# A graph layer and sparse experts kernel: tile 0 selected ahead of the tables, the third tile's W1 loaded early, the first layer in halves of W1

## The chip, the cores and the metric

One core of a Trainium2 chip. The metric is device time in microseconds (us) of one execution, the median of three runs. "The trace" is that of one profiled execution of the kernel before.

## The reference, cut

625 rows of 512 features go through four steps, each on a layer norm of the sum so far and added to it: a graph convolution over 20,000 edges with a linear layer, a small fixed network on a few columns, three graph layers of 512 x 512, and last the part that matters here, a routed network of 16 experts:

```python
for d in range(4):                       # a tree of depth 4 gives each row one of 16 experts
    sel = take_along_axis(xf @ Wr[off:off + cnt].T + br[off:off + cnt], leaf[:, None], 1)[:, 0]
    leaf = leaf * 2 + (sel > 0)
...
h = gelu(xf @ w1 + bb1)                  # W1: 16 x 512 x 2048
y = h @ w2 + bb2                         # W2: 16 x 2048 x 512
acc = acc + m[:, None] * y               # m: the rows of this expert
```

## The kernel before

Five engines run their own instruction lists and wait on semaphores; nothing is planned at run time but what follows. One expert's W1 and W2 are 4 MB each, float32. The kernel computes each expert for its own rows only. A **tile** is one expert with up to 64 rows, and one expert of the 16, the one with the most rows, may have 96 (`more`, tile 14, with matmuls of its own, `first_b` and `second_b`). With these inputs there are 16 tiles, in pairs `p`, `b`; the last pair stands behind the loop. Tiles 0 and 1 are always experts 0 and 1 (`FIXED`), so their weights are loaded at the start of the program; which expert the later tiles are stands in a table (`tab`, `s_table`) that VectorE works out from the routing.

Ahead of tile 0 VectorE ranks the rows by expert, works out the table, and from each row's rank the place of each row, from which `sel` (L1259, semaphore `s_sel`) selects tile 0's 64 rows: TensorE multiplies it with the normed rows (L885), VectorE copies them (L1306), TensorE transposes them (L878, `turn_rows`), VectorE copies the result (L1301, `copy_inputs`). The rows of the later tiles are fetched by GpSimd with a gather from a copy in DRAM (L426). It needs row numbers, `rows_i` (`s_idx`), which come from maps of slots on VectorE (L1308 to L1319), 40 small matmuls on TensorE (L894) and nine steps on VectorE (to L1328).

A tile on TensorE: first layer (L913), 16 matmuls into two PSUM banks, `h` 0 and 1, two for each bank and each of the four row blocks `k` of W1 (the trace counts a float32 matmul as two); transposes of the hidden values (L930) after VectorE's copy (L1338); bias (L947); transposes of the next tile's rows (L878); second layer (L961) in quarters `q`, each behind GELUs on ScalarE (L599). ScalarE copies the result (L611) and GpSimd adds it to the output with a scatter (L433), for which it first picks the row numbers (L420).

There are two buffers for W1 and W2 (`w1_sb`, `w2_sb`). SyncE issues four loads of 2 MB a tile, in order: the two halves `j` of W1, the two halves of W2, each as soon as the tile that used this buffer, two tiles earlier, has read that half (`s_w1u`, `s_h`, `s_l2`). All go through one queue.

The functions that the diff touches, as they stood:

Of the kernel before, what the change touches and what calls it, by code (L numbers as in the profile page):

```python
# [62 lines left out]
FIXED = 2  # L63
# [7 lines left out]
def build(nc, x, src, dst, Wconv, bconv, Wlin, blin, Wa, ba, Ws, bs, Wg, bg, Wr, br, W1, b1, W2, b2, out):  # L71
    ctx = ExitStack()
    with ctx:
# [110 lines left out]
        in_tile = C[:, :, :].rearrange("p c n -> p (c n)")[:, 0:(TAB + 2) * NCH].rearrange("p (t c) -> p t c", c=NCH)  # L184
        tok_tile = C[:, :, :].rearrange("p c n -> p (c n)")[:, 160:160 + (TAB + 2) * NCH].rearrange("p (t c) -> p t c", c=NCH)
        slots = C[:, :, :].rearrange("p c n -> p (c n)")[:, 320:320 + NCH * SA].rearrange("p (c s) -> p c s", c=NCH)
        slotsB = C[:, :, :].rearrange("p c n -> p (c n)")[:, 640:640 + NCH * SB_].rearrange("p (c s) -> p c s", c=NCH)
        rows_f = C[:, :, :].rearrange("p c n -> p (c n)")[:, 960:960 + 3 * (TAB + 2)].rearrange("p (a t) -> p a t", a=3)
        rows_i = C[:, :, :].rearrange("p c n -> p (c n)")[:, 1060:1060 + 3 * (TAB + 2)].bitcast(I32).rearrange("p (a t) -> p a t", a=3)
        row_in, row_inB, row_outB, *row_out = (C[:, :, :].rearrange("p c n -> p (c n)")[:, 920 + i:921 + i].bitcast(I32) for i in range(5))  # L190
        row_inB = row_inB[0:2 * SB_, :]
        half_ofB = C[:, :, :].rearrange("p c n -> p (c n)")[:, 940:941]
        spos = C[:, :, :].rearrange("p c n -> p (c n)")[:, 930:930 + NCH]
# [3 lines left out]
        b1_nat = G[0:2 * NE, 0:HID // 2]  # L197

        b1T = G[:, 1536:1536 + NE * (MH + 1)].rearrange("p (e m) -> p e m", e=NE)
        b1T_flat = G[:, 1536:1536 + NE * (MH + 1)]  # L200
        bT = [G[:, 1824 + b * (MH + 1):1824 + (b + 1) * (MH + 1)] for b in range(2)]
        b2_rows = G[:, 1024:1024 + DIM]
# [19 lines left out]
        s_w1 = [sem(f"w1_in{b}") for b in range(2)]  # L222
# [53 lines left out]
        def _(sp):  # L276
# [41 lines left out]
            for b in range(2):  # L318
                for j in range(2):
                    sp.dma_start(w1_sb[b][:, 2 * j:2 * j + 2, :],  # L320
                                 W1[b, j * 256:(j + 1) * 256, :].rearrange("(p r) n -> p r n", r=2)).then_inc(s_w1[b], 16)
# [18 lines left out]
            sp.dma_start(b1_nat, b1.rearrange("e (h n) -> (e h) n", h=2)).then_inc(s_b1, 16)  # L340
# [12 lines left out]
            with sp.Fori(0, last) as p:  # L353
                for b in range(2):
                    done = 2 * p + b + 1
                    e = sp.value_load(tab[0:1, bass.ds(done + 1, 1)], min_val=0, max_val=NE - 1)
                    for j in range(2):
                        if j == 0:
                            sp.wait_ge(s_w1u, (done - 1) * (KD - 1) + 2)
                        else:  # L360
                            sp.wait_ge(s_h, done * 2)
                        sp.dma_start(w1_sb[b][:, 2 * j:2 * j + 2, :],
                                     W1[bass.ds(e, 1), j * 256:(j + 1) * 256, :].rearrange("a (p r) n -> p (a r) n", r=2)).then_inc(s_w1[b], 16)
                    for h in range(2):
                        sp.wait_ge(s_l2, 4 * (done - 1) + 2 * h + 2)
                        sp.dma_start(w2_sb[b][:, 8 * h:8 * h + 8, :],
                                     W2[bass.ds(e, 1), h * HID // 2:(h + 1) * HID // 2, :].rearrange("a (p m) n -> p (a m) n", p=128)).then_inc(s_w2[b][h], 16)
# [256 lines left out]
        def _(pe):  # L624
# [277 lines left out]
            def tile(p, b, end=False):  # L902
# [476 lines left out]
```

## Time and profile before

| | |
|---|---|
| three runs, us | 628.8, 629.48, 632.06; median 629.48 |
| profiled execution, us | 632.86 |
| its span, first to last instruction, us | 630.9 |
| TensorE matmuls busy | 549.9 us, 87% of the span |
| VectorE, ScalarE, GpSimd busy | 191.2, 162.4, 62.1 us |
| mean granted TensorE clock | 0.96 |
| read from HBM | 142.38 MB |

The span is the program's own time, and the time of an execution is measured around it. Busy shares are averages over stages of very different kinds: the graph steps up to about 285 us, the routing up to 312 us, and the tiles.

### The profile page before, as it was taken

What the parts mean: (1) busy time and instruction counts of PE and PEld (TensorE: products, weight loads), DVE (VectorE), ACT (ScalarE), POOL (GpSimd) and SP (SyncE); (2) the same over time, 40 slices, a digit from 0 to 9 for tenths busy, and PEclk for the clock granted to TensorE, in tenths of its full rate; (3) what the DMA queues carried; (4) which work ended last, traced back from release to release, by engine and by line L of the source; (5) the groups of instructions that cost most, each with busy time, mean ns of one, the idle gap of its engine ahead of it and who ended that gap; (6) DMA issues with size and microseconds to landing.
All of it is one profiled execution on the core that took longest, in us unless ns stands there. A gap on an engine that the chain in (4) does not pass through costs nothing.

```text
span 630.9 us, 9966 instructions
## 1 busy us (share of the span) xinstructions
PE 549.9 (87%) x3098; PEld 288.6 (46%) x3098; DVE 191.2 (30%) x597; ACT 162.4 (26%) x548; POOL 62.1 (10%) x88
## 2 busy tenths in 40 slices
PE   2877787889899999998599999978898788987994
PEld 1544555543447466444355555524444244443352
DVE  5997776661520100266611111100111001110100
ACT  1667777111201011003022222211222012210311
POOL 3000000030000000000021121111101111011021
PEclk9979999999999999999799999988999799897998
DMA  5169900000201010023069999999999999999940
GB/s 116 13 229 431 404 3 16 18 0 1 84 3 65 0 66 0 10 60 104 1 245 422 420 425 419 426 424 426 428 426 418 422 429 425 420 422 424 428 157 5
DMA packets 24917, 145.66 MB, mean 231 GB/s; under 512 B 10303, under 2 KB 12553, under 8 KB 16706
## 3 DMA queue, kind: packets, MB, share of 16 engines
q1 hardware_dynamic: 21698, 142.91, 55.1%
q0 software_dynamic: 3200, 2.50, 2.0%
q8 instruction: 11, 0.18, 0.1%
q14 instruction: 8, 0.07, 0.0%
HBM read 142.38 MB, written 4.72 MB: 233 GB/s over the span
## 4 chain that ended last, share of the span: by engine, by line
PE 53%; DMA 24%; DVE 8%; ACT 6%; issue 5%; ACTq 2%; POOL 0%; SPq 0%; DVEq 0%; POOLq 0%
DMA w<-in_L_ffn_W 24%; PE P L913 15%; PE P L809 8%; PE P L961 7%; PE P L819 7%; PE P L828 3%; ACT H L513 2%; ACT H L507 2%; PE P L663 2%; PE P L930 2%; DVE stats L1085 2%; PE P L772 1%; PE P L771 1%; PE P L768 1%; PE P L785 1%
## 5 line engine op out<-in xcount | busy, mean ns | idle before, releaser
L913 PE MATMUL P<-w,H 128*64 128x512 f32 x512 | 132.2, 663 | 25.3 <-DMA w<-in_L_ffn_W 24.8
L961 PE MATMUL P<-w,FB 128*64 128x256 f32 x1024 | 114.3, 381 | 0.0
L599 ACT ACTIVATE FB<-P,G 128x64 f32<-128x64 f32 x256 | 55.8, 329 | 179.1 <-PE P L930 179.1
L1338 DVE COPY H<-P 128x512 f32<-128x512 f32 x32 | 22.1, 692 | 259.5 <-PE P L913 259.5
L961 PEld LDWEIGHTS P<-w,FB 128*64 128x64 f32 x1024 | 72.0, 137 | 37.4 <-issue 2.9
L913 PEld LDWEIGHTS P<-w,H 128*64 128x64 f32 x512 | 39.1, 151 | 98.6 <-issue 78.7
L663 PE MATMUL P<-H 125*125 125x500 bf16 x176 | 60.0, 418 | 18.5 <-ACT H L513 17.9
L1067 DVE TENSOR_SCALAR H<-iota,small 125x626 bf16<-125x626 f16 x176 | 60.1, 381 | 14.2 <-issue 8.9
L809 PE MATMUL P<-G,XT 128*125 128x512 f32 x120 | 52.0, 592 | 0.0
L663 PEld LDWEIGHTS P<-H 125*125 125x125 bf16 x176 | 25.4, 144 | 44.5 <-ACT H L513 30.6
L819 PE MATMUL P<-C,H 125*128 125x313 f32 (+1 forms) x160 | 42.4, 425 | 0.0
L664 PE MATMUL P<-H 125*125 125x127 bf16 x176 | 40.2, 229 | 0.0
L1185 DVE TENSOR_SCALAR H<-P,dis_c 125x512 f32<-125x512 f32 x15 | 11.3, 752 | 83.8 <-PE P L809 83.8
L507 ACT ACTIVATE H<-iota,small 125x126 bf16<-125x126 f16 x88 | 30.4, 392 | 23.5 <-issue 15.0
L819 PEld LDWEIGHTS P<-C,H 125*128 125x128 f32 x160 | 30.2, 189 | 12.5 <-issue 1.0
L809 PEld LDWEIGHTS P<-G,XT 128*125 128x125 f32 x120 | 22.4, 188 | 27.8 <-issue 27.5
L420 POOL COPY C<-C 128x1 int32 (+2 forms) x33 | 6.6, 200 | 280.4 <-ACT XT L611 91.8
L513 ACT ACTIVATE H<-H,ones 125x126 bf16<-125x126 bf16 x88 | 30.7, 392 | 5.6 <-PE P L664 0.3
L611 ACT ACTIVATE XT<-P 128x256 f32<-128x256 f32 x16 | 6.1, 383 | 82.2 <-PE P L961 82.2
L433 POOL DMA_INDIRECT out<-XT,C x16 | 25.6, 1602 | 14.5 <-POOL C L420 14.5
L575 ACT ACTIVATE XT<-P,bg_c 128x313 f32<-128x313 f32 (+1 forms) x16 | 8.3, 522 | 67.9 <-PE P L819 67.9
L664 PEld LDWEIGHTS P<-H 125*125 125x125 bf16 x176 | 25.8, 147 | 0.0
(283 smaller groups left out, 435.5 us busy)
## 6 DMA issues: line engine op xcount, KB each, us to landing
w<-in_L_ffn_W SPq DMA_DIRECT2D x64, 2048.0 KB, 29.1
G<-in_L_gnn_W SPq DMA_DIRECT2D x3, 1024.0 KB, 5.3
xs<-in_x SPq DMA_DIRECT2D x1, 1120.0 KB
out<-xs SPq DMA_DIRECT2D x5, 224.0 KB
normed_rows<-xn SPq DMA_DIRECT2D x5, 224.0 KB
out<-XT,C POOLq DMA_INDIRECT x17, 10.7
H<-in_L_gnn_W_conv SPq DMA_DIRECT2D x1, 256.0 KB, 9.1
XT<-in_L_gnn_W_lin SPq DMA_DIRECT2D x1, 256.0 KB, 2.8
```

The lines of the kernel that those rows point to most:

```text
L433: nc.gpsimd.indirect_dma_start(out=out.rearrange("t (g n) -> (t g) n", g=2), out_offset=bass.IndirectOffsetOnAxis(ap=row_out[b], axis=0), ...
L507: near = nc.scalar.activation(sqd[0:NC, j, :], iota[0:NC, even:even + DW], ACT.Square, bias=ef[0:NC, 1, j, bass.ds(lo_g + u, 1)], scale=-1.0)
L513: nc.scalar.activation(D[0:NC, j, :], sqd[0:NC, j, :], ACT.Relu, bias=ones[0:NC, 0:1], scale=-1.0).then_inc(s_dhot, 1)
L599: g = nc.scalar.activation(hT[:, m, :], P[:, 3 + rd, c * SA:(c + 1) * SA], ACT.Gelu, bias=bT[b][:, m:m + 1])
L663: nc.tensor.matmul(P[0:NC, b0, 0:GROUP], hot, S[0:NC, j, 0:GROUP], start=False, stop=False, skip_group_check=True)
L664: nc.tensor.matmul(P[0:NC, b0 + 1, 0:LAST], hot, S[0:NC, j, GROUP:GROUP + LAST], start=False, stop=False, skip_group_check=True).then_inc( ...
L809: mm = nc.tensor.matmul(P[0:NC, c, :], XTn[:, k, c * NC:(c + 1) * NC], Gw[:, k, :], start=(k == 0), stop=(k == KD - 1))
L819: mm = nc.tensor.matmul(P[:, (5 + g) % 8, 0:b - a], Hn[0:NC, c, m * 128:(m + 1) * 128], C[0:NC, c, a:b], start=(c == 0), stop=(c == NCH - 1))
L913: mm = nc.tensor.matmul(P[g * SA:(g + 1) * SA, h, :], xT[b][:, k, :], w1a[:, k, h, g], start=(k == 0), stop=(k == KD - 1))
L961: mm = nc.tensor.matmul(P[g * SA:(g + 1) * SA, 7, 0:256], hT[:, m, :], w2_sb[b][:, m, g * 256:(g + 1) * 256], start=False, stop=(m == MH - 1))
L1067: hot = ts(S[0:NC, j, 0:NPAD], iota[0:NC, :], ef[0:NC, 0, j, bass.ds(lo_g + u, 1)], None, ALU.is_equal)
L1338: nc.vector.tensor_copy(h_sb[:, t, :].rearrange("p (r n) -> p r n", r=4), P[:, t, :].rearrange("p (n r) -> p r n", r=4)).then_inc(s_hc, 1)
```

## The change

Six edits.

1. **Tile 0 first.** `sel` is made right after the ranks, from the rank among expert 0's rows alone (`rank0`). The rows of tile 0 are copied and transposed while VectorE goes on with the table. The warm-up matmuls ahead of it go.
2. **Tables beside tile 0.** The slot maps and row numbers (`number_rows`) are made by VectorE after tile 0's two hidden copies; their matmuls (`slot_tokens`) stand in the middle of tile 0's second layer, and the transposes of tile 1's rows at tile 0's end.
3. **The third tile's W1 early.** Tile 2 is always expert 2 (`FIXED = 3`). Its W1 is loaded in four pieces of 1 MB into G, C, xs and xn, as these arrays fall free; `maps`, the biases and b2 move elsewhere for that. Of tiles 0 to 3 the code is written out.
4. **The loads' order.** With W1 of tile 2 out of the way, the buffer that tile 0 leaves is filled with W1 of tile 4. The first loads are written out, the loop begins at pair 2.
5. **The first layer in halves of W1.** Both banks take the first half of W1, then both the second; each half has a semaphore (`s_w1[b][j]`). The 96-row expert's matmuls follow after both.
6. **GpSimd picks a scatter's row numbers before it waits for the result.**

```diff
-FIXED = 2
+FIXED = 3
...
+        w1_two = [G[:, 0:HID]] + [a[:, :, :].rearrange("p c n -> p (c n)")[:, 0:HID] for a in (C, xs, xn)]
...
+            def first_of_two(k):
+                j, r = k // 2, k % 2
+                sp.dma_start(w1_two[k], W1[2, j * 256:(j + 1) * 256, :].rearrange("(p r) n -> p r n", r=2)[:, r, :]).then_inc(s_w1_two, 16)
+
+            first_of_two(0)
             sp.wait_ge(s_b2z, 1)
...
+            sp.wait_ge(s_ga, 4 * KD + NCH)
+            sp.dma_start(b1_nat, b1.rearrange("e (h n) -> (e h) n", h=2)).then_inc(s_b1, 16)
+            first_of_two(1)
+            sp.wait_ge(s_ost, 16 * 2 * NCH)
+            first_of_two(2)
+            sp.wait_ge(s_xst, 16 * 2 * NCH)
+            sp.wait_ge(s_xrow, 1)
+            first_of_two(3)
             sp.wait_ge(s_table, 1)
...
+            load_w1(4, 0, user=0)
+            load_w2(2, 0)
+            load_w1(3, 1, user=1)
+            load_w2(3, 1)
+            load_w2(4, 0)
+            load_w1(5, 1, user=3)
+            load_w2(5, 1)
+            with sp.Fori(2, last) as p:
                 for b in range(2):
+                    load_w1(2 * p + b + 2, b, user=2 * p + b)
+                    load_w2(2 * p + b + 2, b)
...
                 pick(row_out[b], 0, i, count)
+                hold(s_ycp, i + 2)
...
-            keep_warm(4, xn[0:NC, 0, :], bank=4)
             pe.wait_ge(s_sel, 1)
...
-                for k in range(KD):
-                    first_a(0, k)
+                for j in range(2):
+                    first_ready(j)
+                    for h in range(2):
+                        for k in (2 * j, 2 * j + 1):
+                            first_a(h, k)
                 if more:
                     pe.wait_ge(s_xTBc, 1)
-                for k in range(KD):
-                    first_a(1, k)
-                    if more:
+                    for k in range(KD):
                         first_b(k)
-                    if k == 0:
-                        pe.wait_ge(s_hc, 2 * i + 1)
-                        turn(3, 0).then_inc(s_hT, 1)
+                pe.wait_ge(s_hc, 2 * i + 1)
+                turn(3, 0).then_inc(s_hT, 1)
...
                 for q in range(1, 4):
+                    if first and q == 2:
+                        slot_tokens()
                     second_a(q)
+                if first:
+                    pe.wait_ge(s_xr, 16)
+                    turn_rows(1)
...
+            rank, not0, rank0 = sv(0, NCH, NE), sv(90, NCH), sv(100, NCH)
+            link(ts(not0[0:NC, :], leaf[0:NC, :, 0], -EMPTY, EMPTY, ALU.mult, ALU.add))
             dve.wait_ge(s_rank, 1)
...
+            link(tt(rank0[0:NC, :], rank[0:NC, :, 0], not0[0:NC, :], ALU.add))
+            tt(sel[0:NC], iota[0:NC, 0:SA].unsqueeze(1).to_broadcast([NC, NCH, SA]),
+               rank0[0:NC, :].unsqueeze(2).to_broadcast([NC, NCH, SA]), ALU.is_equal).then_inc(s_sel, 1)
```

What the edits move, on three engines. TensorE around tile 0's start: the selection of its rows, their transposes, the slot matmuls and the first layer; before:

```order
284 L885 MATMUL P<-xn,XT 64x256 [waits tile0_selector_ready]
285 L885 MATMUL P<-xn,XT 64x256 x9
286 L878 MATMUL P<-ident,XT 128x128 [waits tile0_rows_copied]
287 L878 MATMUL P<-ident,XT 128x128
288 L894 MATMUL P<-C 64x28 [waits slots_ready]
289 L894 MATMUL P<-C 64x28 x9
290 L894 MATMUL P<-C 32x28 x30
291 L898 TENSOR_LOAD npairs_t [waits table_ready]
```

and now, with the first layer's wait for the second half of W1:

```order
285 L908 MATMUL P<-ident,XT 128x128 [waits tile0_rows_copied]
286 L908 MATMUL P<-ident,XT 128x128
287 L952 MATMUL P<-w_0,H 64x512 [waits tile_copied,w1_in0_0,b2_in,b2_cleared]
288 L952 MATMUL P<-w_0,H 64x512 x7
289 L952 MATMUL P<-w_0,H 64x512 [waits w1_in0_1]
290 L952 MATMUL P<-w_0,H 64x512 x7
291 L969 MATMUL P<-ident,H 128x128 [waits hidden_copied]
```

The slot matmuls and the wait for the table have left the place between the transposes and the first layer. The slot matmuls stand now in tile 0's second layer (L1000), and behind it a wait for the gather ahead of tile 1:

```order
299 L1000 MATMUL P<-w_0,FB 64x256 [waits gelu_done]
300 L1000 MATMUL P<-w_0,FB 64x256 x7
301 L927 MATMUL P<-C 64x28 [waits slots_ready]
302 L927 MATMUL P<-C 64x28 x9
303 L927 MATMUL P<-C 32x28 x30
304 L1000 MATMUL P<-w_0,FB 64x256 [waits gelu_done,w2_in0_1]
305 L1000 MATMUL P<-w_0,FB 64x256 x7
306 L1000 MATMUL P<-w_0,FB 64x256 [waits gelu_done]
307 L1000 MATMUL P<-w_0,FB 64x256 x7
308 L908 MATMUL P<-ident,XT 128x128 [waits tile_rows_in]
309 L908 MATMUL P<-ident,XT 128x128
310 L952 MATMUL P<-w_1,H 64x512 [waits w1_in1_0,tile_copied]
```

Before, tile 1's rows were transposed in the middle of tile 0, as every later tile's still are in the tile before it. On SyncE, the first loads of the stream with what each waits for (w_0 and w_1 are the two buffers, of W1 by L378, of W2 by L386):

```order
89 L378 ISA [waits w1_rows_used]
90 L378 DMA w_0<-in_L_ffn_W 128x4096
91 L378 ISA [waits hidden_bank]
92 L378 DMA w_0<-in_L_ffn_W 128x4096
93 L383 TENSOR_LOAD small
94 L383 ISA x2
95 L386 ISA [waits expert_out]
96 L386 DMA w_0<-in_L_ffn_W 128x4096
97 L386 ISA [waits expert_out]
98 L386 DMA w_0<-in_L_ffn_W 128x4096
99 L372 TENSOR_LOAD small
```

The kinds of wait are as before; the first pair of loads here brings W1 of tile 4 where it brought that of tile 2. VectorE ahead of the selector, now:

```order
292 L1284 TENSOR_SCALAR small<-small 125x5
293 L1286 COPY small<-P 125x80 [waits ranks,dve_chain]
294 L1287 COPY small<-P 128x16
295 L1288 TENSOR_TENSOR small<-small 125x5 [waits dve_chain]
296 L1289 TENSOR_TENSOR XT<-iota,small 125x320 [waits dve_chain]
```

Before, the selector stood behind the 19 rows that begin with the copy of the counts (L1236).

## Rows read from the trace of the kernel before

**Rows 1.** The page: granted TensorE clock and DMA engines' share, 40 slices

```profile
PEclk9979999999999999999799999988999799897998
DMA  5169900000201010023069999999999999999940
```

**Rows 2.** The chain of waits from 387 us: start, length, what

```profile
387.07 28.69 DMA w<-in_L_ffn_W
...
547.56 30.23 DMA w<-in_L_ffn_W
577.84 7.15 PE P L913 x20
```

**Rows 3.** DMA issues by line: count, KB each, median us to landing

```profile
w<-in_L_ffn_W SPq DMA_DIRECT2D x64, 2048.0 KB, 29.1
...
G<-in_L_ffn_b SPq DMA_DIRECT2D x1, 128.0 KB, 2.4
XT<-normed_rows,C POOLq DMA_INDIRECT x16, 2.4
```

**Rows 4.** The weight buffers' loads: us to landing, least, median, most

```profile
DMA to landing us min/median/max: 7.5/29.1/39.5
```

**Rows 5.** Timeline from the ranks to the first gather: start, length, engine, what

```profile
294.61 0.18 DVE L1236 COPY small<-P 128x16 f32<-128x16 f32 x1
...
299.12 0.49 DVE L1259 TENSOR_TENSOR XT<-iota,small 125x320 f32<-125x320 f16 x1
...
299.66 2.38 PE L885 MATMUL P<-xn,XT 125*64 125x256 f32 x20 [0.47 <-DVE XT L1259]
...
303.62 0.17 DVE L1287 CAST small<-small 1x28 int32<-1x28 f32 x1
...
304.88 0.42 DVE L1306 COPY XT<-P 128x256 f32<-128x256 f32 x1
...
305.36 0.51 PE L878 MATMUL P<-ident,XT 128*128 128x128 f32 x2 [3.31 <-DVE XT L1306]
305.90 0.42 DVE L1301 COPY H<-P 128x256 f32<-128x256 f32 x1 [0.60 <-PE P L878]
...
309.00 0.32 DVE L1319 TENSOR_TENSOR C<-iota,C 125x160 f32<-125x160 f16 x1
...
309.38 2.48 PE L894 MATMUL P<-C 125*64 125x28 f32 x80 [3.52 <-DVE C L1319]
...
312.29 6.81 PE L913 MATMUL P<-w,H 128*64 128x512 f32 x20 [0.43 <-issue]
...
313.58 0.23 DVE L1328 TENSOR_SCALAR C<-C 64x28 int32<-64x28 f32 x1
...
315.06 1.26 POOL L426 DMA_INDIRECT XT<-normed_rows,C  x1 [1.00 <-POOL C L420]
```

**Rows 6.** Timeline: tile 1's first layer on TensorE, and loads on SyncE

```profile
320.89 2.08 SPq L362 DMA_DIRECT2D w<-in_L_ffn_W  x2
...
330.76 4.46 PE L913 MATMUL P<-w,H 128*64 128x512 f32 x20
...
337.00 2.04 SPq L362 DMA_DIRECT2D w<-in_L_ffn_W  x2
343.63 3.79 SPq L366 DMA_DIRECT2D w<-in_L_ffn_W  x2
```

**Rows 7.** A stretch of 3 us in tile 0's first layer

```profile
core 0: us, PE busy (x) PEld busy (x) DVE busy (x) ACT busy (x) POOL busy (x), PEclk, DMA share, GB/s
312.30:315.30 3.00, 3.00 (x8) 1.00 (x10) 1.34 (x8) 0.00 (x0) 0.42 (x2) 0.50 0.00 0
```

**Rows 8.** Timeline of the end: tiles 14 and 15

```profile
592.51 0.65 PE L947 MATMUL P<-G 128*64 128x256 f32 x4
...
606.13 4.51 PE L913 MATMUL P<-w,H 128*64 128x512 f32 x20
...
622.51 0.38 ACT L611 ACTIVATE XT<-P 128x256 f32<-128x256 f32 x1 [5.32 <-PE P L961]
...
624.18 1.57 POOL L433 DMA_INDIRECT out<-XT,C  x1 [0.86 <-POOL C L420]
```

More of the change, by code:

```diff
@@ L193, in build @@
[L193 to L202, printed above, removed]
+        maps = C[:, :, :].rearrange("p c n -> p (c n)")[:, HID:NCH * NPAD]
+        in_tile, tok_tile = (maps[:, i * 140:i * 140 + (TAB + 2) * NCH].rearrange("p (t c) -> p t c", c=NCH) for i in range(2))
@@ L905, in tile, with first_ready @@
                 more = end and b == 0
+                first = isinstance(p, int) and i == 0
                 pe.wait_ge(s_xTc, i + 1)
-                pe.wait_ge(s_w1[b], 32 * (p + 1))
-                w1a = w1_sb[b][:, :, :].rearrange("p k (h n g r) -> p k h g n r", h=2, g=2, r=4)
+                usual = not isinstance(p, int) or p != 1 or b == 1
+                blocks = [w1_sb[b][:, k, :] for k in range(KD)] if usual else w1_two
+                w1a = [w.rearrange("p (h n g r) -> p h g n r", h=2, g=2, r=4) for w in blocks]
+                def first_ready(j):
+                    if not usual:
+                        pe.wait_ge(s_w1_two, 16 * KD)
+                    elif b or isinstance(p, int):
+                        pe.wait_ge(s_w1[b][j], 16 * (p + 1))
+                    else:
+                        pe.wait_ge(s_w1[b][j], 16 * p)
                 def first_a(h, k):
                     for g in range(2):
-                        mm = nc.tensor.matmul(P[g * SA:(g + 1) * SA, h, :], xT[b][:, k, :], w1a[:, k, h, g],
+                        mm = nc.tensor.matmul(P[g * SA:(g + 1) * SA, h, :], xT[b][:, k, :], w1a[k][:, h, g],
                                               start=(k == 0), stop=(k == KD - 1))
@@ L948, in tile @@
                                      b2_rows[:, g * 256:(g + 1) * 256], start=True, stop=False)
-                if not (end and b):
+                if not (first or end and b):
                     pe.wait_ge(s_xr, 16 * i + 16)
@@ L986, in tile @@
                     mm.then_inc(s_l2B, 1)
-            with pe.Fori(0, last) as p:
+            for p in range(2):
+                for b in range(2):
+                    tile(p, b)
+            pe.wait_ge(s_table, 1)
+            last = pe.value_load(npairs_t[0:1, 0:1], min_val=NE // 2 - 1, max_val=MAX_PAIRS - 1)
+            with pe.Fori(2, last) as p:
                 for b in range(2):
@@ L1321, in _ @@
-            link(ts(half_ofB, part, float(SB_), -2.0, ALU.is_ge, ALU.add))
-            dve.wait_ge(s_rows, 1)
-            for which, per, of in ((0, 2.0, half_of), (1, 4.0, quarter_of), (2, 2.0, half_ofB)):
-                rows = 2 * SB_ if which == 2 else 128
-                v = P[0:rows, 7, which * 32:which * 32 + TAB + 2]
-                link(ts(rows_f[0:rows, which, :], v, 0.5, EMPTY, ALU.is_lt, ALU.mult))
-                link(stt(rows_f[0:rows, which, :], v, per, rows_f[0:rows, which, :], ALU.mult, ALU.add))
-                ts(rows_i[0:rows, which, :], rows_f[0:rows, which, :], of[0:rows, :], None, ALU.add).then_inc(s_idx, 1)
@@ L1343, in tile_copies @@
                     nc.vector.tensor_copy(h_sb[:, 2, :].rearrange("p (r n) -> p r n", r=4), P[:, 2, :].rearrange("p (n r) -> p r n", r=4)).then_inc(s_hBc, 1)
+                if isinstance(p, int) and i == 0:
+                    number_rows()
                 if not (end and b):
                     copy_inputs(i + 1, 1 - b)
-            with dve.Fori(0, last) as p:
+            for b in range(2):
+                tile_copies(0, b)
+            with dve.Fori(1, last) as p:
                 for b in range(2):
```

143 lines of the change are left out of this document (75 added, 68 removed).

## The prediction

> **What bounds the kernel now.** I read the page's slices first. From the 21st slice on the DMA engines are at nine tenths or more until nearly the end, while TensorE's digit in the granted clock falls now and then [rows 1]: it runs out of work there. The chain of waits says on what: from 387 us on it goes from one 2 MB weight load to the next, and tile 14's first matmul starts 0.05 us after its W1 is complete, at 577.8 us [rows 2]. Between the landing at 415.76 us (387.07 plus 28.69) and the one at 577.79 us lie 32 loads, so one load takes 162.0 / 32 = 5.06 us, and a tile's four take 20.3 us [rows 2, 3]. TensorE needs 16.1 us for a tile where nothing holds it, which is the distance of the same load's issue in tiles 0 and 1, 320.89 and 337.00 us [rows 6]. So the kernel has three parts: before tile 0 (ends at 312.29 us [rows 5]), the weight stream, and 53.1 us of TensorE work behind the landing of tile 14's W1 (577.8 to 630.9), in which the last loads are hidden. What counts is when the stream can flow without a gap, how many loads stand in it ahead of tile 14's W1, and those last 53 us.
>
> **Tile 0 earlier.** Before, the selector of tile 0 (L1259) came at 299.12 us, behind a chain of 19 small operations that starts at 294.61; then table (L1287), copies (L1306, L1301), slot maps (L1319) and 40 matmuls with them (L894) came ahead of the first L913 [rows 5]. Now the selector needs the copy of the ranks, the copy of the counts and one addition. No row shows the first and third; small steps here last between 0.18 (L1236) and 0.49 us (L1259), I take 0.24 and 0.2, and 0.15 for one more step ahead of them: 294.61 + 0.15 + 0.24 + 0.22 + 0.2 + 0.49 = 295.9 us. The selection (2.38 us) ends at 298.3 and is hidden under the chain that now follows on VectorE: 295.8 + 4.3 (294.79 to 299.12) = 300.1. Then copy 0.42, transposes 0.51, copy 0.42 with 0.1 of handing over: tile 0 starts at **301.6 us**, 10.7 earlier. The four warm-up matmuls that fall away (0.43 us each) lay in a wait. The biases' load, now issued behind the stores at about 290 us, is needed at 294.5; it landed 2.4 us after its issue before [rows 3], so I cost it at nothing (if late, tile 0's selection moves with it, at most 1 us).
>
> **What tile 0 now carries.** Its first layer is 16 matmuls of 0.43 us, 6.9 (the trace counts each twice). Before, the first 10 took 6.81 us against 4.46 in tile 1, because the clock was at 0.50 there [rows 5, 6, 7]: 2.35 lost, after TensorE had stood still for 3.3 and 3.5 us around L878. Now the pauses there are 2.2 and 0.5 us; the loss lies between 0 and 2.35, I take 1.7. First layer done at 310.2. Three short groups (transposes, bias, transposes; 0.6 each) and half of the second layer (3.6) bring 315.6. The slot maps on VectorE start after the second hidden copy, 310.9, and take 3.0 (L1301's end 306.32 to L1319's end 309.32): 314.0, no wait. The 40 matmuls: 2.5, to 318.1. Now comes the new wait. VectorE makes the row numbers in 1.95 us (311.86 to 313.82), GpSimd needs 1.25 to issue the gather (313.81 to 315.06) [rows 5], which lands 2.4 us later [rows 3]: 323.7 us, while TensorE has ended the second layer at 321.7. Behind the wait stand the transposes (0.51) and the copy of tile 1's inputs (0.45): tile 1 starts at **324.6 us**, against 330.76. So of 10.7 us 6.2 are left there. In GpSimd's queue the gather for tile 2 stands behind this one and tile 14's; it would be issued by 326 us and is wanted at 332.
>
> **The stream.** Loads now are W1(4), W2(2), W1(3), W2(3), W2(4), W1(5), W2(5), then W1 and W2 of 6, 7 and so on, two loads of 2 MB each: 54, not 56. The 4 MB of W1(2) go as four loads of 1 MB into arrays of the graph layers, 1 at 264 us, 2 at 290 to 291 us, 1 after the selection at 298.3; the DMA engines are nearly idle there [rows 1] and tile 2 wants them at 341 us, so they cost nothing, and if late they would have 38 us. W1(4)'s first half is issued after tile 0's first eight matmuls. Each issue waits for TensorE, and at first TensorE is the slower one. The last gap is at the 9th load, the first of W2(4), which waits for half of tile 2's second layer. Tile 2 starts at 324.6 + 16.1 + 0.9 = 341.6 (0.9 for the clock after the 2 us pause at 322; bounds 0 and 2.35). Such a load is issued 12.9 us after its tile's start (330.76 to 343.63), and lands 7.5 us later when the queue is empty [rows 4, 6]: 341.6 + 20.4 = 362.0 us, where a queue without a gap would have brought it at 357. From there loads follow without a gap, since TensorE frees four places in 16.1 us and four loads take 20.3. The second half of W1(14) is the 48th load: 362.0 + 39 x 5.063 = **559.5 us**, against 577.8. That is 10.1 us for two loads fewer ahead of it and 8.2 for the earlier stream.
>
> **Behind it.** Tile 14's first half of W1 lands 5.1 us before the second, at 554.4, and TensorE is free then (tile 13's last weights land at 549.4, and 3.5 us of matmuls follow). Before, from the landing of the whole to the bias matmuls at 592.51 took 14.7 us [rows 8]. Now the half that is left takes 3.45, the 96-row expert's own 16 matmuls 4.0 (they were 4 groups of 1.0), a transpose group 0.6: 8.05, so 6.6 us less. From the bias to tile 15's start 13.6 as before (592.51 to 606.13): 581.2. W1(15) has landed by 579.8 and W2(15) by 590.0, wanted at 590 and 593. In tile 15 the copy of the second bank, for which TensorE waited 0.4 us, is covered by the first bank's transposes: 0.6 less. GpSimd picks the rows before it waits for the result: from L611's start to L433's 1.67 us before, 0.6 now, 1.0 less. From L433's start to the end 6.7 stay. 581.2 + 15.8 + 0.6 + 6.7 = **604.3 us** of span. The profiled execution had a span of 630.9 and took 632.86; its span shrinks by 26.6. The median of the runs is 629.48, 3.4 below the profiled one; less 26.6 it is 602.9. Forecast: **603 us**.
>
> **A rule that speaks against the halves.** The profile's loss at L913 of 2.35 us came after pauses of over 3 us, with the clock granted at 0.50, that is 1.2 of 2.4 GHz [rows 7]. With halves TensorE pauses more often: after each half (1.7 us), and for W2. The Trainium skill, "TensorE: Matmul & The Clock Gate", section HAM oscillation, tells of a kernel whose waits for DMA between steps left every step at the half clock. By that rule the sum would be that of the rival below; by the rows, shorter pauses should cost less, not more. The trace of before agrees with it only for the long pauses.
>
> **Rivals.** (a) Tile 1's start is later than I think, by the gather or the clock: every us goes straight to the end, since the 9th load hangs on it. If tile 1 started at 330.76 as before, the end would be 6.2 later, 609. For it: the gather, row numbers and three engines' handovers stand in one line. Against: each has a row. (b) The pauses of the halves keep the clock low in tile 14: 3.4 to 6.9 us are then lost of the gain of 6.6 behind the landing, 606 to 609. (c) Slower than before: the clock stays low through all DMA-bound tiles. A tile at 1.2 GHz would be up to 14.6 us longer than 16.1 (its matmuls doubled), 30.7; TensorE instead of the stream would set tiles 6 to 15, and 26.6 us of gain are used up when a tile's mean goes over 20.3 + 2.7 = 23 us, which is at about half of its work at the low clock. At the full price: 10 x 10.4 = 104 us more than forecast, 707. Against: before, pauses of 2 and 4 us a tile cost at most one low stretch each. (d) The change does something else: expert 2 is now excluded from being the one of 96 rows; had it more than 64 rows, two more tiles of 20.3 us would come, 643 us. The inputs give expert 14 73 rows, expert 2 28 and no other over 54. (e) The early loads or tables disturb nothing but win nothing, only the two loads fewer count: 629.5 - 10.1 = 619.
>
> **How the numbers follow.** Forecast as worked out, 599.5 to 606: 0.57. (a) 0.2, (b) 0.14, (e) 0.05, (c) 0.03, of which 0.01 would end within 0.5%, (d) 0.01. Low end of the likeliest: full clock in tiles 0 and 1 (-2.6), so 600, with 1 us of slack in the small steps and chips, 599. High end with (a) or (b): 609, and 5.1 for 5.06 us a load adds 1.5: 610. The range 598.5 to 610.5 leaves out part of (a), (b) and the rest. A measurement of this kernel tells 0.5%, 3 us, from no change. Faster 0.96, same 0.01, slower 0.03.
>
> **What would show it.** In the changed kernel's profile: selection near 296 us, first L952 near 301.6, second tile's near 324.6 with a wait for the gather ahead of it; a dip in the DMA share between 350 and 357 us and none after; one 2 MB load per 5.06 us; TensorE's second half of tile 14 at about 559.5 with the clock at 1.0; 44.8 us from there to the end. A later tile 1 or a gap in the stream after 362 us makes me wrong upwards; a slope other than 5.06 us, either way; low clock in the halves, upwards.

## The result and the profile after

The change made the kernel faster: 614.37 us (median of four runs, 611.82 to 615.86) against 630.06 us (four runs) for the kernel before, a ratio of 0.9725, 95% interval 0.9699 to 0.9751. That is 15.7 us less by these two medians, whose quotient is 0.9751; by the ratio of 0.9725 it is 17.3 us. I had forecast 603 with a range up to 610.5, so the forecast is wrong: the kernel is slower than I said. The profiled execution, the fastest of the four, took 611.82 us with a span of 609.9; I had said 604.3.

First the page's slices, granted TensorE clock and DMA share, to be laid beside [rows 1]:

```profile
PEclk9979999999999999999897999999999999999998
DMA  6169900100202010024686979999999999999980
```

The low digits of the clock all along the second half are gone; behind the 3rd slice only the 20th (8), the 22nd (7) and the last are left. The DMA digits rise from the 18th slice on, with the early pieces of W1, and then show two dips, at the 22nd slice (320 to 335 us, 6) and the 24th (350 to 366 us, 7).

The timeline around tile 0 (start, length, engine, what, and in brackets the idle time ahead and what ended it):

```profile
294.92 0.49 DVE L1289 TENSOR_TENSOR XT<-iota,small 125x320 f32<-125x320 f16 x1
...
295.47 4.07 PE L914 MATMUL P<-xn,XT 125*64 125x256 f32 x20 [0.22 <-DVE XT L1289]
...
301.42 7.09 PE L952 MATMUL P<-w,H 128*64 128x512 f32 x32 [0.79 <-DVE H L1318]
...
313.69 1.93 PE L927 MATMUL P<-C 125*64 125x28 f32 x80
314.05 5.69 SPq L386 DMA_DIRECT2D w<-in_L_ffn_W  x2
...
317.35 0.23 DVE L1384 TENSOR_SCALAR C<-C 64x28 int32<-64x28 f32 x1
...
318.83 1.26 POOL L458 DMA_INDIRECT XT<-normed_rows,C  x1 [1.00 <-POOL C L452]
...
326.32 0.70 PE L908 MATMUL P<-ident,XT 128*128 128x128 f32 x2 [7.09 <-DMA XT<-normed_rows,C]
...
327.54 5.63 PE L952 MATMUL P<-w,H 128*64 128x512 f32 x20 [0.52 <-DVE H L1318]
```

The selector stands at 294.92 instead of 299.12, and tile 0's first layer starts at 301.42 instead of 312.29 [rows 5]. At the other end of tile 0 TensorE stands still for 7.09 us: the gather of tile 1's rows is issued at 318.83 and nothing else is left to do. SyncE's row at 314.05 is W2(2), one of its two loads ahead of the gather and the other 0.6 us behind it. The chain of waits shows its whole length, and how it goes on (the same columns without the brackets):

```profile
318.83 7.44 DMA XT<-normed_rows,C
...
327.54 8.21 PE P L952 x32
...
344.85 6.87 PE P L952 x32
...
528.03 37.08 DMA w<-in_L_ffn_W
565.15 3.65 PE P L952 x16
...
586.06 7.20 PE P L952 x32
...
602.12 0.39 ACT XT L641
...
603.37 1.57 POOL out L466
```

The gather needed 7.44 us from issue to landing. The next gather of the same kind, for tile 2, is issued at 328.31, when the four loads issued until then have almost landed (the last at 330.04), and it lands 2.6 us later (its row in the timeline, and the landing of this one issue):

```profile
328.31 1.05 POOL L458 DMA_INDIRECT XT<-normed_rows,C  x1 [0.85 <-POOL C L452]
DMA to landing us min/median/max: 2.6/2.6/2.6
```

The DMA engines' share is 0.08 and less from 328.0 to 330.0 us and was about 1 while the first gather was in flight. Tile 1's first layer took 8.21 us, tile 2's 6.87. The second half of tile 14's W1 landed at 565.11 (528.03 plus 37.08), and TensorE took it up 0.04 us later, exactly the link that [rows 2] showed. From there to the end of the span it is 44.8 us.

Granted clock in two stretches (busy time and instructions of each engine, then clock, DMA share, GB/s):

```profile
323.10:329.70 6.60, 2.87 (x8) 1.08 (x10) 0.42 (x1) 0.00 (x0) 1.42 (x3) 0.50 0.71 293
330.00:606.00 276.00, 250.70 (x1818) 126.94 (x1814) 28.94 (x61) 59.91 (x272) 46.72 (x59) 1.00 0.94 389
```

The granted clock fell to 0.50, that is 1.2 of 2.4 GHz, in the wait for the gather and stayed there into tile 1. From 330 us on it is at 1.00 throughout.

And the load on which the last gap hangs, the first of W2(4), on SyncE's queue:

```profile
357.54 3.78 SPq L386 DMA_DIRECT2D w<-in_L_ffn_W  x2
```

It landed 9.0 us after this issue, at 366.5. I had forecast 362.0.

### The profile page after: what moved, and what is told of

The parts are those of the page before. It is cut to its first block, busy times and chain, and to the rows that moved or that the text cites. A ratio compares the mean times of both kernels' runs of the same rounds, so it can differ in the third digit from the quotient of the medians.

```text
span 609.9 us, 9957 instructions
## 1 busy us (share of the span) xinstructions
PE 532.0 (87%) x3090; PEld 284.6 (47%) x3090; DVE 191.5 (31%) x600; ACT 160.8 (26%) x548; POOL 62.4 (10%) x88
## 4 chain that ended last, share of the span: by engine, by line
PE 58%; DMA 20%; DVE 8%; ACT 6%; issue 5%; ACTq 2%; POOL 0%; DVEq 0%; SPq 0%; POOLq 0%
DMA w<-in_L_ffn_W 18%; PE P L952 13%; PE P L1000 11%; PE P L839 8%; PE P L849 7%; PE P L858 4%; ACT H L537 2%; PE P L693 2%; ACT H L543 2%; PE P L969 2%; DVE stats L1134 2%; DMA XT<-normed_rows,C 1%; PE P L986 1%; PE P L802 1%; PE P L801 1%
## 5 line engine op out<-in xcount | busy, mean ns | idle before, releaser
L952 PE MATMUL P<-w,H 128*64 128x512 f32 x480 | 108.6, 600 | 17.1 <-DMA w<-in_L_ffn_W 15.8
L1000 PE MATMUL P<-w,FB 128*64 128x256 f32 x1024 | 115.6, 381 | 5.5 <-DMA w<-in_L_ffn_W 5.5
L629 ACT ACTIVATE FB<-P,FB 128x64 f32<-128x64 f32 x256 | 54.3, 362 | 156.2 <-PE P L969 156.2
L1000 PEld LDWEIGHTS P<-w,FB 128*64 128x64 f32 x1024 | 72.0, 137 | 43.9 <-issue 10.7
L952 PEld LDWEIGHTS P<-w,H 128*64 128x64 f32 x480 | 35.9, 138 | 81.6 <-issue 60.5
```

The costliest lines, as they stand in the source:

```text
L629: g = nc.scalar.activation(hT[:, m, :], P[:, 3 + rd, c * SA:(c + 1) * SA], ACT.Gelu, bias=bT[b][:, m:m + 1])
L952: mm = nc.tensor.matmul(P[g * SA:(g + 1) * SA, h, :], xT[b][:, k, :], w1a[k][:, h, g], start=(k == 0), stop=(k == KD - 1))
L1000: mm = nc.tensor.matmul(P[g * SA:(g + 1) * SA, 7, 0:256], hT[:, m, :], w2_sb[b][:, m, g * 256:(g + 1) * 256], start=False, stop=(m == MH - 1))
```

## The experiments

Each was timed against the kernel before on its own chip. To compare two of them I take the difference of their ratios times 631 us; each ratio is known to about 0.003, so such a difference is known to about 2.6 us. The medians of before in the three groups were 632.04, 630.97 and 632.02 us. One trace is kept of each, and where the clock falls differs between executions of one kernel, so times taken from two traces differ by that as well.

**The changed kernel again (e1)**, unedited, as the neighbour of the next three.

> The changed kernel once more, beside the others on one chip. Theory A (the gather for tile 1 meets the weight stream): the gather issued near 319 us lands 7 to 8 us later while loads are in flight, tile 1 starts near 327.5, the span is 610 to 613, the ratio to the kernel before 0.970 to 0.975. Theory B (the gather of tile 1 is slow by itself, its first use after a long rest): the same here. If the run spread explains the gap of 11 us to the forecast, this run should come out nearer 605.

Measured: 614.99 us, ratio 0.9734 (0.9704 to 0.9764). The gather took 7.6 us (318.77 to 326.41), tile 1 started at 327.67, the ninth load landed at 368.1, the end was at 611.8. Everything stands as in the first trace, but here the clock stayed low for 10.2 us after the wait instead of 6.8, and tile 2 starts 1.7 us later for it (346.38). So the distance to the forecast is not the spread of the runs: a second median stands 12 us above 603. The two theories on the gather expected the same of this run; the next one parts them.

**Nothing in the air when the gather is issued (e2).** W2(2), issued during tile 0's second half, waits until tile 1's rows are in.

```diff
                 for h in range(2):
                     sp.wait_ge(s_l2, 4 * (i - 2) + 2 * h + 2)
+                    if isinstance(i, int) and i == 2 and h == 0:
+                        sp.wait_ge(s_xr, 16)
```

> The first load of W2 for tile 2 is held back until tile 1's rows have landed; nothing else changes. Theory A: with the loads ahead drained the gather lands 2.5 to 4 us after its issue, tile 1 starts at 322.5 to 324.5, and since the ninth load hangs on tile 1 the span ends 3 to 5 us earlier, 605 to 607, although two loads are issued up to 7 us later. Theory B: the gather still takes 7.4 us, tile 1 stays at 327.5, the span stays at 610 or grows a little. Rival C (the stream is full from its start, and what counts is its first load): loads 3 and 4 later by 7 us move the whole stream, the span grows by up to 7 us, to 617.

Measured: 610.51 us, ratio 0.9656 (0.9633 to 0.9679), 4.9 us below e1. The gather in GpSimd's timeline:

```profile
323.47 1.26 POOL L460 DMA_INDIRECT XT<-normed_rows,C  x1 [1.00 <-POOL C L454]
```

And TensorE's timeline behind it, with its wait and tile 1's first layer:

```profile
326.50 0.51 PE L910 MATMUL P<-ident,XT 128*128 128x128 f32 x2 [2.33 <-DMA XT<-normed_rows,C]
327.53 2.79 PE L954 MATMUL P<-w,H 128*64 128x512 f32 x12 [0.52 <-DVE H L1320]
```

The same gather now lands 3.0 us after its issue, TensorE waits 2.33 us instead of 7.1, and the clock does not fall. In this execution the clock was low from 298.5 to 308.7 us, so that the gather was issued 4.7 us later than in e1, and still tile 1 started at the same time. So it is the loads in flight, not the gather itself, that make the 7.4 us. The 2.6 us of tile 2's gather in the changed kernel says the same, and a slow first use (theory B) is ruled out by e6 and e8 below: there the same first gather, issued ahead of the loads, took 3.16 and 2.94 us. The price is a stream that starts later: W2(2) is issued 12.7 us later, and the ninth load, though issued at 356.4, lands only 10.1 us behind that, at 366.5.

**Tile 1 without a gather (e3).** Tile 1's rows are selected by TensorE like tile 0's, with a selector and ten matmuls ahead of tile 0. No gather, and W1(2)'s last piece waits for the second selection.

```diff
+            for c in range(NCH):
+                for g in range(2):
+                    mm = nc.tensor.matmul(P[g * SA:(g + 1) * SA, 3, 0:256], sel1[0:NC, c, :], xn[0:NC, c, g * 256:(g + 1) * 256],
+                                          start=(c == 0), stop=(c == NCH - 1))
+            mm.then_inc(s_xrow, 1)
...
-            gather(1, 1)
```

> Tile 1's rows are selected by matmul like tile 0's, from the rank among expert 1's rows, so no gather stands ahead of tile 1; this puts 20 small matmul instructions (1.6 to 2.4 us) and three small VectorE steps ahead of tile 0. Theory A: tile 0 starts at 302.5 to 304, tile 1 at 320.5 to 322.5 with no wait, the ninth load lands 5 to 8 us earlier than 366.5, the span is 602 to 605, ratio 0.958 to 0.963. Theory C (the first load sets the stream): the span grows by the 1 to 2.5 us that tile 0 starts later, to 611 to 613.

Measured: 606.42 us, ratio 0.9598 (0.9562 to 0.9635), 8.6 us below e1. TensorE's timeline from tile 0's transposes over the second selection to the two tiles' starts:

```profile
301.74 0.70 PE L910 MATMUL P<-ident,XT 128*128 128x128 f32 x2 [3.07 <-DVE XT L1326]
302.37 3.54 PE L923 MATMUL P<-xn,XT 125*64 125x256 f32 x20
305.75 7.04 PE L959 MATMUL P<-w,H 128*64 128x512 f32 x32
...
323.60 1.89 PE L959 MATMUL P<-w,H 128*64 128x512 f32 x8
```

Tile 0 starts 4.4 us later than in e1 and tile 1 4.1 us earlier, right behind tile 0 and with no idle time ahead of it. The ninth load landed at 361.1 and tile 14's second half of W1 at 560.7, close to the 559.5 of the record. The ratio came as theory A had it, but not the times in it: I had expected tile 0 at 302.5 to 304 and tile 1 at 320.5 to 322.5. The second selection took 3.54 us, most of it at the half clock, and the transposes ahead of it waited 3.07 us for VectorE.

**The first layer not in halves (e4)**: the order of the kernel before within a tile, all else as changed.

```diff
                 for j in range(2):
                     first_ready(j)
-                    for h in range(2):
-                        for k in (2 * j, 2 * j + 1):
-                            first_a(h, k)
+                for k in range(KD):
+                    first_a(0, k)
...
```

> The changed kernel with the first layer in the old order, both halves of W1 awaited at its start, the transposes of bank 0 inside it. By the forecast's sum the halves are worth 6.6 us in tile 14 and 0.6 in tile 15: the distance from the landing of tile 14's W1 to the end grows from 44.8 to 52, the span to 617, ratio 0.980 to 0.985, and the clock falls in the pauses of 4 us ahead of the tiles. Rival (halves cost as much in clock as they win): no more than 2 us of difference.

Measured: 623.68 us, ratio 0.9857 (0.9833 to 0.9881), 7.8 us above e1. The page's slices of clock:

```profile
PEclk9979999999999999999897999999998889888998
```

And the chain from tile 14's W1 on, with pieces left out:

```profile
540.27 30.98 DMA w<-in_L_ffn_W
...
571.39 6.21 PE P L952 x20
577.59 1.00 PE P L961 x8
...
616.38 1.57 POOL out L466
```

The way behind the landing is 51.8 us (571.25 to 623.04) instead of 44.8. TensorE waits once a tile for the whole of W1, for 1.7 to 4.1 us, 17.3 us in the seven tiles from 448 us on, and the clock falls for 3.4 us in the last six of them, tile 14 among them, behind pauses of 1.9 to 4.1 us. A pause of 1.65 us, the first, left it at 1.00.

**W1 of the third tile in the stream (e5)**: the four early pieces go, and the order of loads is the old one with 56 loads.

```diff
-            first_of_two(0)
...
-            with sp.Fori(2, last) as p:
+            with sp.Fori(0, last) as p:
```

> The changed kernel without the early load: W1 of tile 2 is the first load of the stream again, 56 loads in the old order; all else stays. The forecast's sum counts the early load at two loads of 5.06 us: the end 10 us later, ratio 0.988 to 0.990. Rival D (the early load is partly lost again, since the buffers then stand full and the stream pauses until tile 2 has read half of W2): here the ninth load waits for tile 2's first layer only, so the stream has no pause from the fifth load on, the ninth lands near 362, the second half of W1 for tile 14, now the 50th, near 570.5, 5 to 6 us later than the 565.1 of the changed kernel; ratio 0.981 to 0.984.

Measured: 621.03 us, ratio 0.9813 (0.9784 to 0.9843), 5.0 us above e1. The fifth load on SyncE's queue:

```profile
337.84 0.33 SPq L371 DMA_DIRECT2D w<-in_L_ffn_W  x1
```

It is issued 5.7 us after tile 1's start and is the last one that leaves a gap; from there the stream is full, while in the changed kernel it still has a gap at the ninth, 30.0 us after tile 1's start (357.54 less 327.54). With T for tile 1's start, tile 14's second half lands at T + 243.8 here (332.18, 575.99) and at T + 237.6 in the changed kernel (327.54, 565.11). Two loads fewer bring 6.2 us by that, 5.0 by the ratios, and not 10.1: the gap at the ninth load takes the rest. That is rival D with its ratio; its 570.5 us for tile 14's second half did not come, because in this execution the clock fell near 301.8 us, tile 0's first layer took 9.80 us and not 7.09, and tile 1 started 4.6 us later than in the changed kernel's trace.

**Tables ahead of tile 0 (e6)**: `slot_tokens` and `number_rows` stand ahead of tile 0 as before, and tile 1's rows are transposed inside tile 0 again; the rest is changed.

```diff
+            slot_tokens()
             for p in range(2):
...
+            number_rows()
             for b in range(2):
                 tile_copies(0, b)
...
```

> The changed kernel with slot maps, their matmuls and the row numbers ahead of tile 0 again, so tile 0 starts at 311 to 312 instead of 301.4, but the gather for tile 1 is issued near 314 with no load in flight and tile 1's rows are turned inside tile 0. Theory A: tile 1 starts at 329 to 331 without a wait of 7 us and at the full clock, its second layer at the same time as in the changed kernel within 1.5 us; the span changes by 0 to +3 us, ratio 0.973 to 0.978: tables beside tile 0 bring next to nothing. The forecast's sum, in which they bring 6 us, would give a ratio of 0.983.

Measured: 612.97 us, ratio 0.9704 (0.9677 to 0.9732); 1.9 us below e1, which the intervals don't tell from none. The gather:

```profile
316.29 1.26 POOL L458 DMA_INDIRECT XT<-normed_rows,C  x1 [1.02 <-issue]
```

Tile 0 starts at 313.0, 11.6 us later than in e1, but tile 1 only 2 us later (329.65) and tile 2 0.8 us earlier (345.62). The gather is issued ahead of the first load and lands in 3.2 us, hidden by tile 0, and tile 1 runs at the full clock. So what tables beside tile 0 gain at its start is spent again in the wait behind it, and tile 14's second half of W1 lands at 566.4, against 566.7 in e1. The ratio lies below the 0.973 to 0.978 that theory A gave, and far from the 0.983 of the forecast's sum.

**Warm-up matmuls in the wait (e7, e10)**: 13, then 6 matmuls with 512 columns that nobody reads.

```diff
                 if first:
+                    for _ in range(13):
+                        nc.tensor.matmul(P[:, 2, 0:DIM], ident[:, :], w2_sb[1][:, 0, :], start=True, stop=True)
                     pe.wait_ge(s_xr, 16)
```

> The changed kernel with 13 more matmuls of 0.43 us (into a bank that nobody uses, 5.6 us) between tile 0's second layer and the wait for the gather, which is 7.1 us long, so that they are hidden. Theory: the clock fell because TensorE stood still there; now it stays up, tile 1's first layer takes 7.0 instead of 8.2 us and more, and the end comes 1 to 3 us earlier, span 607 to 610, ratio 0.968 to 0.972, with less spread between runs. Rival: the clock falls all the same, the end stays within 0.5 us.

Measured: 616.51 us, ratio 0.9768 (0.9738 to 0.9798). TensorE's timeline (it counts each matmul twice):

```profile
321.28 11.43 PE L1026 MATMUL P<-w,ident 128*128 128x512 f32 x26
...
333.45 7.09 PE L952 MATMUL P<-w,H 128*64 128x512 f32 x32 [0.52 <-DVE H L1320]
```

I had counted 0.43 us for one; that is what one of a tile's first layer takes, which uses 64 columns of weights. These, with 128, took 0.88 us (11.43 / 13), so they ran 4.0 us past the gather, which landed at 328.67, and tile 1 started at 333.45, 5.8 us later than in e1. Part of the 5.8 is this execution's own: its tile 0 had a first layer of 8.69 us and ended 2.2 us later. Tile 1 ran at the full clock, and the end was only 2 us later.

> Six full-width matmuls with a result that nobody reads, in the wait for tile 1's gather; the run with thirteen showed 0.88 us for one, so that these take 5.3 us of the 7.1 us and stay hidden. Theory (the clock at half behind that wait costs tile 1's first layer 1.1 us, and more in the tiles behind it): granted clock at 1.0 through tile 1, its first layer 7.1 us, end 1 to 3 us ahead of the repeat of the changed kernel, ratio 0.967 to 0.972. Rival: the loads take the gain back before the ninth, ratio 0.972 to 0.974, the same as the changed kernel.

Measured: 614.50 us, ratio 0.9721 (0.9689 to 0.9753), the same as the changed kernel. The time is the rival's, but its reason was not put to the test: the clock fell all the same, and there was no gain that the loads could have taken back. TensorE's timeline:

```profile
319.62 5.42 PE L1026 MATMUL P<-w,ident 128*128 128x512 f32 x12
327.06 0.70 PE L908 MATMUL P<-ident,XT 128*128 128x128 f32 x2 [2.03 <-DMA XT<-normed_rows,C]
328.28 9.85 PE L952 MATMUL P<-w,H 128*64 128x512 f32 x32 [0.52 <-DVE H L1320]
```

And a stretch of it, with the clock of 0.50 behind the engines' busy times:

```profile
327.10:333.80 6.70, 6.18 (x16) 2.00 (x18) 0.42 (x1) 0.00 (x0) 3.06 (x4) 0.50 0.22 73
```

They kept the clock up while they ran, and then it fell at 327.05, after a pause of 2.03 us, and tile 1's first layer took 9.85 us. In e2 a pause of 2.33 us in the same place did not do that. The kernel before has such a pair too: a pause of 2.01 us ahead of the first layer at 455.97 us was followed by 0.50, one of 3.56 us ahead of tile 14's at 577.84 was not. Which pauses make the clock fall is not settled by their length.

**The kernel before with halves alone (e8).**

```diff
-                pe.wait_ge(s_w1[b], 32 * (p + 1))
...
+                for j in range(2):
+                    pe.wait_ge(s_w1[b][j], 16 * (p + 1))
+                    for h in range(2):
+                        for k in (2 * j, 2 * j + 1):
+                            first_a(h, k)
...
```

> The kernel before with the first layer in halves of W1 alone. By the forecast's sum the landing of tile 14's W1 stays at 577 to 579 us and the rest shrinks from 53.1 by 6.6 in tile 14 and 0.6 in tile 15, to 46: ratio 0.987 to 0.990. If the gain needs the other edits, or the clock falls in the added pauses, less than 3 us, 0.995 or more.

Measured: 622.40 us, ratio 0.9862 (0.9837 to 0.9888), that is 8.7 us below the kernel before. The page's slices of clock:

```profile
PEclk9979999999999999999889999999999999999998
```

And the chain at its end:

```profile
537.92 36.97 DMA w<-in_L_ffn_W
...
574.93 3.65 PE P L912 x16
...
595.85 7.02 PE P L912 x32
...
611.73 0.39 ACT XT L611
...
613.40 1.57 POOL out L433
```

The way behind the landing is 45.1 us against 53.1 before, and the clock no longer falls in the tiles that wait for weights. The landing itself did not stay at 577 to 579 us, as I had expected, but came at 574.9, against 577.8 before.

**The second selection inside tile 0 (e9)**: as e3, but its ten matmuls stand behind tile 0's first layer and its VectorE steps behind tile 0's.

```diff
+                if first:
+                    pe.wait_ge(s_sel, 2)
+                    for c in range(NCH):
+                        for g in range(2):
+                            mm = nc.tensor.matmul(P[g * SA:(g + 1) * SA, 5, 256:512], sel1[0:NC, c, :], xn[0:NC, c, g * 256:(g + 1) * 256],
+                                                  start=(c == 0), stop=(c == NCH - 1))
+                    mm.then_inc(s_xrow, 1)
```

> Tile 1's rows are selected by matmuls as in e3, but its VectorE steps stand behind the b1T copies and its ten matmuls stand inside tile 0, behind the first layer's first half; W1(2)'s fourth piece is issued behind the next W1. Theory A (the wait of 7.1 us for the gather, and the low clock behind it, are what tile 1 lost against the forecast): tile 0 starts at 301.4 as in the changed kernel, not 305.75 as in e3; the ten matmuls add about 2.2 us to tile 0; there is no wait of over 1 us ahead of tile 1, whose first layer starts at 321.5 to 322.5, tile 2 at 338 to 340; W1(14)'s second half lands between 555 and 560.5; end at 600 to 605, ratio to the kernel before 0.952 to 0.960. Rival (the loads set the end from the ninth load on, and 39 of them at 5.09 us are the same from there): like e3, 0.960, end at 605 to 606, since tile 1 of e3 was already at 323.6.

Measured: 607.91 us, ratio 0.9610 (0.9577 to 0.9644), not told from e3. Its steps in TensorE's timeline were as expected:

```profile
301.71 7.09 PE L954 MATMUL P<-w,H 128*64 128x512 f32 x32 [0.79 <-DVE H L1327]
308.59 2.36 PE L987 MATMUL P<-xn,XT 125*64 125x256 f32 x20
...
321.78 1.46 PE L954 MATMUL P<-w,H 128*64 128x512 f32 x6
```

The ratio is the one that the rival named, 0.960, and just outside theory A's 0.952 to 0.960. Tile 1 starts at 321.78, 1.8 us before e3's, tile 2 1.4 us before, and the span of the profiled execution is 604.4, 1.5 us shorter. The runs don't show these 1.5 us. Both versions beat the changed kernel; I can't say which of the two is better.

**The picks back behind the wait (e11).**

```diff
+                    hold(s_ycp, i + 2)
...
-                hold(s_ycp, i + 2)
```

> The last edit alone is undone: the waits of GpSimd ahead of its picks and scatters stand where they stood before. Prediction on record: the edit is worth 1.0 us at the end (from the last step of VectorE or ScalarE to the last scatter). What the two traces showed of it: 0.4 us. So the ratio would be 0.974 to 0.975, within the interval of the changed kernel, and in the trace the way from the start of the last bias step to the start of the last scatter is 1.67 us, not 1.25.

Measured: 612.72 us, ratio 0.9691 (0.9654 to 0.9728), so undoing the edit costs nothing that can be measured; the ratio is even below the 0.974 to 0.975 expected, within what two ratios can differ by. At the end of the timeline:

```profile
602.51 0.38 ACT L643 ACTIVATE XT<-P 128x256 f32<-128x256 f32 x1 [4.86 <-PE P L1002]
603.14 0.18 POOL L452 COPY C<-C 128x1 int32 x1 [13.85 <-ACT XT L643]
604.18 1.57 POOL L465 DMA_INDIRECT out<-XT,C  x1 [0.86 <-POOL C L452]
```

From ScalarE's step to the scatter it is 1.67 us here and 1.25 in the changed kernel, so the edit takes 0.42 us from the chain.

## Why the forecast was wrong

Between 602.9 and 614.37 us lie 11.5 us. 5.6 of them are in the sum that gave the span (609.9 against 604.3), and 5.9 in the step from the profiled execution to the median. Neither alone would have left the range up to 610.5: 602.9 with 5.6 is 608.5, with 5.9 it is 608.8. The terms of the span can be placed one by one; of the step to the median the runs show the size, and only a part of the cause.

- **Tile 0's start held**: 301.42 against 301.6. The selection took 4.07 us at the half clock, not 2.38, and it was luck that it stayed hidden: it ended at 299.54, and VectorE was free to copy its rows at 299.60. The warm-up matmuls that went had taken 3.70 us for four in the kernel before, right ahead of the selection, not 0.43 each. **What tile 0 carries held, on the short side**: the first layer ran at the full clock, slot matmuls took 1.93 us, and TensorE was done at 319.22, not 321.7. The 1.7 us that I had given to the clock were not lost here, and that too is luck of the execution: here the clock fell near 295.7 us and was back by 299.2, while in e2 it fell at 298.5 and in e5 and e7 near 301.8 us, and tile 0's first layer took 9.67, 9.80 and 8.69 us there, against 7.09 in the changed kernel, e1, e9, e10 and e11.
- **The first step that failed is the new wait, "which lands 2.4 us later [rows 3]: 323.7 us".** The gather was issued 2.5 us earlier than forecast and took 7.44 us, not 2.4, so it landed at 326.27. e2 shows the cause: without loads in flight it takes 3.0, in e6 3.2, and tile 2's in the changed kernel's own trace 2.6. The row I read it from says x16 and 2.4, but the trace of before knows the landing of one gather alone, issued at 317.44, 3.4 us ahead of the first load [rows 6]; and that one is tile 14's second, smaller gather (L441, 64 pieces of 1 KB, not 128). That row is a price without load; the change puts the gather between the loads. The scatters, the same kind of transfer, landed in a median of 10.7 us in the trace of before between 340 and 600 us, and would have warned me. The Trainium skill, "DMA: Bandwidth & Descriptors", section Queues, rings and completion order, says that each DMA engine takes packets by turns from the queues that have work; the 3.0 us without and 7.44 us with loads agree with that.
- **Tile 1's start** was therefore 327.54 and not 324.6: 2.6 us from the gather, 0.4 from the transposes at the half clock and the handing over. This was my rival (a), which had put its whole price at 6.2 us.
- **From tile 1 to tile 2** 17.1 us, forecast 17.0. Where nothing holds it a tile takes 16.0, so the low clock took 1.1 us in this execution, forecast 0.9; in e1 it took 2.7.
- **The ninth load, a second term that was too small**, was issued 12.86 us into tile 2, as forecast, but landed 9.0 us later, not 7.5. The 7.5 was the least of [rows 4]. In e1 it was 8.9. That is 1.5 us. The load came at 366.5 in place of 362.0 (2.9, 0.1 and 1.5).
- **The slope** was 198.6 us for 39 loads, 5.09 each, forecast 5.063: 1.1 us more. (From [rows 1] I read nine tenths for the DMA engines from the 21st slice on; its digit is 6, and they begin with the 22nd. Nothing hangs on it.)
- **Behind the landing, 44.8 us held**, and so did what the halves bring there: e8 alone has 8.0 of the 8.3. That the sum is exact is luck, since its parts are not: the pick was worth 0.4 us and not 1.0, the way from the bias to tile 15 was 13.1 and not 13.6, tile 15 took 16.1 (586.06 to 602.12) and not 15.8. Rivals (b) and (c) fell, and (d) and (e) with their 643 and 619 us: with pauses of 0.9 to 1.6 us the clock stayed at 1.00 through the six tiles, 9 to 14, that wait for weights.
- **What the earlier stream and the two loads are worth was mis-sized**, both and in sum. The record has 8.2 and 10.1 us, 18.3 together; the landing of tile 14's W1 came 12.7 us earlier (577.79 less 565.11). e5 has 5 to 6 for the two loads, e6 nothing for tables beside tile 0. Of the 17 us of the whole by the ratios, 8 to 9 are the halves (e4, e8), 5 the early W1 (e5), and 3 or 4 are left for all the rest, little more than the 2.6 us that one such difference is known to. No run has the new order of loads by itself.
- **The second step that failed is the one from the profiled execution to the median, "3.4 below the profiled one; less 26.6 it is 602.9".** I carried over to the changed kernel that the profiled execution of before was slow for its kernel, by 3.4 us. The profiled execution of the changed kernel was a fast one, 2.55 us below its own median. So 5.6 of the span, 3.4 and 2.5 make the 11.5 us between 602.9 and 614.37. Profiled against profiled the gain is 21.0 us, of medians 15.7. In the eleven experiments the profiled execution lay between 1.8 below and 1.9 above its median; the two of the record lay further out, on opposite sides. Executions of one kernel differ by up to 7 us (604.86 to 611.57 in e3). Each execution's mean granted clock is on record, and in most kernels the slow ones have the lower: spans of 602.9, 602.9, 603.1, 605.9, 606.2 and 609.6 us in e3 with 0.989, 0.989, 0.989, 0.988, 0.987 and 0.979, and 609.9, 612.2, 613.9 and 612.7 in the changed kernel with 0.983, 0.981, 0.978 and 0.977. e6 and e11 don't show it. Two places for it are in the traces, tile 0's first layer (7.09 or up to 9.80 us) and tile 1's (8.21 or up to 9.85 us). That this is the whole spread is not shown, as only the profiled executions have traces.

The rule that I had weighed against the halves (the Trainium skill, "TensorE: Matmul & The Clock Gate", section HAM oscillation) is about waits that leave the next step at the half clock. Here those were the single waits for all of W1, in e4 1.9 to 4.1 us with the half clock behind each of six, and the wait of 7.1 us. I had also read the trace of before as agreeing for long pauses only; it has the half clock behind 2.10 us (at 435.94) and 2.01 us (at 455.97) too. Taking up W1 in halves made two or three pauses a tile of 0.9 to 1.6 us, with more waiting in all (21.3 us from 440 to 570 us against 15.4 in e4), and the clock stayed at 1.00. The halves were a cure for it, not a cause; why, these traces don't settle.

## What to carry to other kernels

The price of a small transfer is read where it will stand, among the loads that will be in flight then, and a median in a list is first asked how many landings it is made of. Work that is moved out of a wait leaves only what the next wait doesn't take: follow the chain until something that no longer depends on it, here the ninth load, and count from there. Where a step waits for a big load, taking it up in parts won twice here, at the end of the chain and by a clock that stayed up. And a forecast of a median is anchored on a median: one profiled execution can lie 2 to 3 us to either side of its own.

## What the runs showed of the hardware

- One gather of 128 pieces of 1 KB: 2.6 to 3.2 us to landing with the queue of loads empty or nearly so (2.6 for tile 2's in the changed kernel, 2.94 in e8, 3.0 in e2, 3.16 in e6), 6.5 to 8.0 for the first one issued among loads (e1, e4, e5, e7, e9, e10, the changed kernel). The scatters with addition: 3.7 us for the changed kernel's first, issued at 330.62 with the queue of loads empty, a median of 10.8 for all 17.
- In the changed kernel six tiles with two or three pauses each of 0.9 to 1.6 us left the clock at 1.00. Pauses of 2.03 us (e10) and 2.33 us (e2) in the same place once ended in the half clock for 6.8 us and once didn't; in the kernel before 2.01 us did and 3.56 us didn't.
- A float32 matmul with 512 columns took 0.88 us with 128 columns of weights (e7) where each of those with 64 columns cost 0.43 in a row of them.
